# A graph layer on one core: x loads, squares and rectifications move between steps, and the two halvings and the zero products change

## What is computed

```python
def reference(x, adj, W, b):             # x 8192x128, adj 8192x8192, W 128x128
    h = jnp.maximum(_layernorm(x, axis=-1), 0.0)
    out = jnp.matmul(adj, jnp.matmul(h, W)) + b
    return x + jax.nn.relu(out)
```

## Time and profile before

| what | value |
|---|---|
| median of 3 runs | 722.28 us (722.16 to 722.79) |
| the profiled execution | 722.6 us, of which its span is 720.8 us |
| PE busy | 715.5 us, 99% of the span |
| DVE, ACT, POOL busy | 620.4, 517.0, 171.5 us |
| read from HBM | 276.89 MB at a mean of 391 GB/s |

### The profile page before, as it was taken

How to read it: one execution, slowest core, us unless ns; L and a number is a source line. 1 busy time by engine, 2 the same in 40 slices (tenths; PEclk the granted TensorE clock), 3 DMA queues, 4 the chain that set the end, 5 groups by cost and what they waited for, 6 DMA issues and landing times.

```text
span 720.8 us, 7916 instructions
## 1 busy us (share of the span) xinstructions
PE 715.5 (99%) x3125; PEld 586.4 (81%) x3125; DVE 620.4 (86%) x387; ACT 517.0 (72%) x394; POOL 171.5 (24%) x99
## 2 busy tenths in 40 slices
PE   9999999999999999999999999999999999999998
PEld 5788888888888888888888888888888888888886
DVE  5899999999999888988789888878888787888885
ACT  2798988888888867766567677677676676766662
POOL 4445455554444402222011000000000000033213
PEclk9999999999999999999999999999999999999999
DMA  9999999999999999999999999999999999999992
GB/s 352 408 409 407 408 412 415 412 416 415 416 414 416 418 415 412 398 374 402 373 412 392 408 409 389 377 401 383 386 392 373 389 394 387 391 404 397 366 400 85
DMA packets 45109, 281.60 MB, mean 391 GB/s; under 512 B 5136, under 2 KB 5776, under 8 KB 31504
## 3 DMA queue, kind: packets, MB, share of 16 engines
q1 hardware_dynamic: 44496, 280.25, 97.5%
q10 hardware_dynamic: 576, 0.85, 0.4%
HBM read 276.89 MB, written 4.19 MB: 390 GB/s over the span
## 4 chain that ended last, share of the span: by engine, by line
PE 97%; DMA 2%; DVE 0%; ACT 0%; SPq 0%; issue 0%; DVEq 0%
PE banks L558 94%; DMA raw<-adj 2%; PE banks L600 2%; PE banks L592 1%; PE banks L585 0%; PE banks L586 0%; PE banks L584 0%; ACT high L378 0%; SPq L244 0%; DVE x_sb L479 0%; DVE x_sb L487 0%; DVEq L150 0%; DVE warm L491 0%; DVEq L478 0%
## 5 line engine op out<-in xcount | busy, mean ns | idle before, releaser
L516 DVE TENSOR_TENSOR low<-raw,high 128x3072 fp32r<-128x3072 f32 (+2 forms) x255 | 574.7, 2276 | 86.4 <-PE banks L558 64.4
L378 ACT ACTIVATE high<-raw 128x3072 fp32r<-128x3072 f32 (+2 forms) x255 | 483.0, 1903 | 190.3 <-DMA raw<-adj 178.4
L558 PE MATMUL banks<-high,h_high 128*128 128x512 f32 x1012 | 271.6, 390 | 1.1 <-ACT high L378 1.1
L558 PE MATMUL banks<-high,h_low 128*128 128x512 f32 x1012 | 271.0, 389 | 0.0
L558 PE MATMUL banks<-low,h_high 128*128 128x512 f32 x1012 | 267.8, 389 | 0.0
L558 PEld LDWEIGHTS banks<-high,h_high 128*128 128x128 f32 x1012 | 189.8, 188 | 41.8 <-ACT high L378 2.0
L558 PEld LDWEIGHTS banks<-low,h_high 128*128 128x128 f32 x1012 | 189.8, 188 | 39.9 <-DVE low L516 0.4
L558 PEld LDWEIGHTS banks<-high,h_low 128*128 128x128 f32 x1012 | 189.9, 188 | 39.5
L330 POOL TENSOR_SCALAR x_sb<-x_sb,bias 128x512 f32<-128x512 f32 x16 | 49.5, 3095 | 419.3 <-DMA x_sb<-x_blocks 419.3
L321 POOL TENSOR_SCALAR z_sb<-x_sb,neg_mean,rstd 128x128 f32<-128x128 f32 x60 | 89.8, 1510 | 1.6
L306 POOL TENSOR_TENSOR rstd<-var_eps,minus_half 128x4 f32<-128x4 f32 (+2 forms) x17 | 31.6, 1861 | 118.3 <-DVE var_eps L421 109.1
(11 more groups left out here) (34 smaller groups left out, 50.1 us busy)
## 6 DMA issues: line engine op xcount, KB each, us to landing
raw<-adj SPq DMA_DIRECT2D x106, 1536.0 KB, 8.9
raw<-adj SPq DMA_DIRECT2D x82, 768.0 KB, 10.5
raw<-adj SPq DMA_DIRECT2D x69, 512.0 KB, 11.8
x_sb<-x_blocks SPq DMA_DIRECT2D x16, 256.0 KB, 8.6
out_blocks<-x_sb SPq DMA_DIRECT2D x15, 256.0 KB, 9.7
x_sb<-x SPq DMA_DIRECT2D x14, 256.0 KB, 11.9
raw<-adj SPq DMA_DIRECT2D x3, 256.0 KB, 6.9
raw<-adj ACTq DMA_DIRECT2D x1, 256.0 KB, 2.7
```

The lines of the kernel that those rows point to most:

```text
L378: nc.scalar.activation(high[:, t % HIGH_SLOTS, cols], raw[:, t % RAW_SLOTS, cols], ACT.Copy).then_inc(high_ready, 1)
L516: nc.vector.tensor_tensor(low[:, t % LOW_SLOTS, cols], raw[:, t % RAW_SLOTS, cols], high[:, t % HIGH_SLOTS, cols].bitcast(F32), ALU.subtra ...
L558: return nc.tensor.matmul(banks[:, FIRST_BANK[g] + c, :], h[:, (t - FIRST_STEP[g]) * DEPTHS[g] + k, :], tile[:, slot, at:at + BANK], start ...
```

## The change

```diff
-WARMING = 8
+WARMING, WARM = 2, 448
 def mean_at(t):
-    return batch_at(t, 1, 3) if t >= 5 else None
+    return batch_at(t, 2, 3) if t >= 6 else None
 def variance_at(t):
-    return batch_at(t, 3, 3) if t >= 7 else None
+    return batch_at(t, 0, 2) if t >= 8 else None
 def rectified_at(t):
-    return 2 if t == 2 else batch_at(t, 3, 2) if t >= 7 else None
+    return {2: 2, 5: 3}.get(t, batch_at(t, 3, 2) if t >= 11 else None)
 def squares_at(t):
-    j = batch_at(t, t % 4, 3) if t >= 6 and t % 4 in (2, 3) else None
-    if j is None:
+    j = batch_at(t, 3, 3) if t % 4 == 3 else batch_at(t, 0, 2)
+    if t < 7 or j is None:
         return None
-    at = BATCHES[j][0] + (t % 4 - 2) * 2
+    at = BATCHES[j][0] + (t % 4 == 0) * 2
...
+        warm = last_sum[:, 0:WARM]
...
-            act.wait_ge(warm_ready, 1)
-            nc.scalar.activation(unread[:, :], warm[:, 0:1], ACT.Square)
+            act.wait_ge(constants_ready, 1)
+            nc.scalar.activation(unread[:, :], minus_half[:, 0:1], ACT.Square)
...
-                if t == 9:
+                if t == 28:
                     dve.wait_ge(h_first_ready, FOUR_PASS)
...
-                nc.tensor.matmul(banks[:, PSUM_BANKS - 1, 0:P], warm[:, :], warm[:, :], ...)
+                nc.tensor.matmul(banks[:, PSUM_BANKS - 1, 0:WARM], warm[:, 0:P], warm[:, :], ...)
```

More of the change, by code:

```diff
@@ L170, in gnn_layer @@
         rstd = sb("rstd", [P, TILES])
-        warm = sb("warm", [P, P])
         unread = sb("unread", [P, 1])
@@ L591, in _ @@
             for _ in range(WARMING):
-                nc.tensor.matmul(banks[:, PSUM_BANKS - 1, 0:P], warm[:, :], warm[:, :], start=True, stop=True)
+                nc.tensor.matmul(banks[:, PSUM_BANKS - 1, 0:WARM], warm[:, 0:P], warm[:, :], start=True, stop=True)
             for t in range(FOUR_PASS):
```

## The result

The changed kernel took 726.64 us (median of 6 runs, 724.28 to 728.4), the kernel before 722.38 (6 runs, 722.15 to 722.79): a ratio of 1.0053, 95% interval [1.004, 1.0065]. It is slower by 4.3 us, where 0.3 us less was forecast. The profiled execution is the longest of the six, 728.4 us (span 726.6), 5.8 above that of before. The other five stand at 724.3, 724.7 and three times 726.6 to 726.7, so what costs the time doesn't strike equally often in each. The measured time lies inside the stated range, but in the part that the range had only for the slower rival.

A forecast was written before the change was run, and what follows sets the result against it. PE was taken to bound the kernel, gapless from 31.59 us, so only the stall before it could be saved. The load's 0.3 us gain and zeros elsewhere gave 722.28 - 0.3 = 722.0 us; 8 in 10 range 721.0 to 731.5.

The forecast's parts named there:

- the slower rival: POOL's scalings come too late for ACT from step 31, costing PE time each round to step 59: 731 us, chance 0.28.
- What bounds the kernel: PE works without a gap from 31.59 us; only the 1.23 us lost just before that can be saved.
- x of batch 4 behind step 5: Moving this load lands step 5 0.7 us earlier but delays step 6; net gain 0.3 us, bounds 0 and 0.7.
- The stall at (5, 2): PE's wait near 30.4 us for this late adj piece, 1.23 us lost; forecast to go.
- The wait forecast at (6, 1): PE waits 0.7 to 0.9 us near 33.3 us for ACT's copy of this piece, the next late one.
- Code packets: With 24 fewer PE instructions at the start, the first packet on queue 8 moves from 28.28 to near 31.0 us.
- Zero products: At the start, two of 448 columns replace eight of 128; a later clock rise could cost 0 to 0.5 us, taken as 0.
- Its cover: The 1.6 us for which the products of step 0 wait for adj anyway, with 1.2 us more in the later stall.
- Squares, mean, early rectification, halves at 0: Lighter ACT and DVE work in steps 5 to 9, 0.8 us more DVE work at step 28; 0 for the total.
- POOL no longer keeps up: Later variance leaves the four scalings no margin at step 31; 1.0 to 1.2 us lost per round, 731 us, chance 0.28.

The follow-up runs named there:

- start alone: Kernel before with only two zero products of 448 columns and ACT's first instruction waiting on POOL's constant: 722.42 us, ratio 1.0001.
- chain back: Changed kernel with x load, mean, squares and variance back at their old steps, the rest of the change kept: 722.39 us, ratio 1.0.
- only batch 4 moved: Kernel before with x load, mean, squares and variance moved for batch 4 alone, plus early rectification and late halves: 721.98 us, ratio 0.9998.
- the chain moved alone: Kernel before with only the change's moves of x load, mean, squares and variance: 730.76 us, ratio 1.0096.
- batches 9 to 16 back: Changed kernel with x load, mean, squares and variance of these batches at old steps: 724.86 us; the same with the old eight zero products: 724.79 us.

## Why the prediction was wrong, point by point

- **What bounds the kernel** was read rightly: nothing behind 31.6 us could save time, only cost some. All of the 6.3 us lies there.
- **x of batch 4 behind step 5.** The stall at (5, 2) went, and PE had gained 0.52 us at step 31, not 0.3. But this isn't shown to be the work of the x load. With the load at its old step, ACT's copy of (5, 2) starts at 29.24 (start alone), 29.46 (rectification and halves alone) and 28.81 us (chain back), and PE doesn't wait there. It starts at 30.49 in the kernel before, where the packet at 28.28 falls ahead of that piece. PE's step 31 starts between 135.2 and 136.1 us in five traces with the load moved, and between 135.3 and 136.0 in five with it unmoved; in the other four, long waits for POOL came before it. The copy of (5, 2) itself started at 29.43, 1.0 later than the 28.4 forecast. The wait forecast at (6, 1) didn't come, since PE started step 2 1.3 us later and so had what it lacked as slack there (by the times; no run tests it). In the kernel with only batch 4 moved, where PE wasn't late, part of the stall did come back, at (6, 0) with 0.58 us, and the median fell by 0.3, which isn't clear of noise.
- **Code packets.** Forecast near 31.0, measured 31.64. In the seven traces with eight zero products the first packet comes at 27.96 to 28.75 us, in the seven with two at 30.43 to 31.64. So its time goes with the number of PE's instructions, as the prediction had it; what the packet holds no trace names.
- **Zero products.** Forecast cost 0 to 0.5, taken as 0. The risk named, records at 0.8 us, happened with two (0.98 and 0.86 us), and step 2 was 1.3 us late. Its cover, the stall at (5, 2), was there, so at the end it cost nothing that the runs can tell (722.42 for the start alone, and 724.79 against 724.86). The text had said that such records would prove it wrong; they didn't touch the end.
- **Squares, mean, early rectification, halves at 0**: right for the rectification and the halves (722.39). One part of it the sum didn't have: the halves now stand right behind the variance of step 28, and the power beside them took 1.01 us instead of 2.47. Wrong for the mean and squares in so far as they were costed apart from the variance; the mean's place is one of POOL's few turns.
- **The step that failed** is the overlap of POOL's work with DVE's: the forecast took the round that ends at step 31 for all later ones, with ACT's wait below the 1.1 us that PE can bear, and gave *POOL no longer keeps up* 0.28. The working for step 31 was right: scalings to end between 133.7 and 134.3, measured 133.89; ACT to wait 0.3 to 0.8 us, measured 0.54. That was in part luck: the power took 1.01 us instead of 2.47, and the four scalings 7.32 instead of 5.41. And the round doesn't repeat. ACT's waits were 0.54, 0.70, 2.80 and 4.36 us, POOL took 9.91 and then 9.66 us where it has 8.46, and PE lost 1.22 us in each of five rounds. My argument against the rival, that step 30 "is fed by landings, which leave DVE short gaps", used gaps that exist only as long as ACT and DVE are ahead, and even with such a gap (0.77 us, the chain moved alone) a power of 4.11 us began the lock. A margin of nothing on a path that feeds back should have been the likeliest case for a loss, not 0.28.
- **The rival's sizes.** Round of 17.3 us forecast, 17.54 measured; 1.0 to 1.2 us a round, measured 1.22. Its sum put the entry at step 31 with seven rounds; it was step 39 with five. So 731 was too high for the change, and the 730.6 to 732.4 of the kernels with part of it are nearer.
- **The shared way to SBUF** (the Trainium skill, GPSIMD Engine Reference, 1. Specifications: POOL shares its SBUF interfaces with VectorE and contends with DVE instructions of two SBUF inputs) agrees with the trace: 0.44 us for a scaling beside a reduction, 4.19 for one inside a row of four subtractions. I had written that by it the slower case would be the rule and not the exception, and gave it too little weight.

## What to carry to other kernels

Where an engine gets its work done only in another's gaps, count the gaps between release and deadline, and ask what becomes of them when the chain runs late: if lateness closes them, one missed turn grows to a steady loss, and the static margin of the kernel before says nothing. The test is a sum over one round: what the other engines take from its result to its next release, and what the bounding engine leaves of the round (here 8.46 us). A step that is moved towards its deadline needs a margin of at least one missed turn, here 1.6 to 2.4 us (POOL's 9.66 and 10.47 against 8.03). And the idle time of the bounding engine can hide such a loss among many small waits; the chain of waits names the engine that sets the round.

## What the runs showed of the hardware that I had not expected

- How long POOL is shut out depends on the seams. A scaling of 128 columns took 0.44 us with DVE outside a subtraction, 1.9 to 2.6 behind one or two seams between subtractions, 4.19 when it began in the second of four in a row (it passed two seams), 5.1 beside three in a row. The power of 128x4 took 1.01 us when DVE paused just behind the variance, mostly 1.9 to 2.6 when a subtraction followed at once, 4.1 to 4.2 in four traces (the kernel before is one), and 7.45 in both kernels with batches 9 to 16 back (at 139.75 us in the first).
- The time at which the first products come to the full granted clock moved by microseconds, and no run here shows why. In the clock records it was 6.9, 9.2, 7.2, 9.5, 5.0, 7.3 and 4.7 us in the seven profiled executions with two zero products of 448 columns, and 4.5 to 6.6 in the seven with eight of 128. Ahead of it the records of 512 columns in the changed kernel came 0.98 and 0.86 us apart, by that pace at 1.2 GHz, and behind it 0.43 (2.4 GHz). The end of the kernel hardly followed it. With the chain back, step 2 began at 17.22 us (15.33 before) and PE then had no wait of its own, so that step 64 began at 270.62 against 270.58: the late start had taken what the stall takes in the kernel before.
